# Gram products of two adapter pairs as four 64x64 blocks in a transformer layer with adapter feed-forwards

## The reference

```python
B, S, D, H = 16, 512, 256, 16            # batches, tokens, width, heads of 16
N, R = 8, 64                             # adapters and their inner width
def ffn(x):
    h = relu(einsum('btd,ndh->nbth', x, W_enc) + b_enc)       # h of all N adapters
    recon = einsum('nbth,nhd->nbtd', h, W_dec) + b_dec
    n = argmin(mean((recon - x) ** 2, axis=(2, 3)), axis=0)    # one adapter per batch
    mid = relu(x @ W_down[n] + b_down[n])
    return x @ W_base + b_base + mid @ W_up[n] + b_up[n]
x = x + 0.5 * ffn(layernorm(x))
x = x + attention(layernorm(x))          # rotary positions, softmax, float32
x = x + 0.5 * ffn(layernorm(x))
```

## Time and profile before

| | |
|---|---|
| Median of 3 runs | 1824.24 us (1820.42 to 1824.45) |
| The profiled execution | 1821.28 us, its span 1819.5 us |
| TensorE busy | 1719.4 us, 95% of the span |
| VectorE busy | 1270.7 us, 70% |
| ScalarE busy | 975.3 us, 54% |
| GpSimd busy | 501.8 us, 28% |
| Mean clock granted to TensorE | 0.969 of full speed |

### The profile page before, as it was taken

The page is one execution under the profiler, slowest core; times in us unless marked ns, Lnnn a source line. Parts: engine busy times, 40 slices in busy tenths (PEclk is TensorE's granted clock), DMA queues, the critical chain, the costliest instruction groups (busy, mean ns, idle before and its releaser), DMA issues.

```text
span 1819.5 us, 26356 instructions
## 1 busy us (share of the span) xinstructions
PE 1719.4 (95%) x9064; PEld 1004.2 (55%) x9064; DVE 1270.7 (70%) x2827; ACT 975.3 (54%) x1954; POOL 501.8 (28%) x665
## 2 busy tenths in 40 slices
PE   5478999999999999999999999999999999999966
PEld 4343555655555565656555565556556555654434
DVE  5558686877768686777868687776868777676521
ACT  2125565564747465564746556474746556474531
POOL 2414042230415133141513224141413304140101
PEclk9688999999999999999999999999999999999986
DMA  4343322333343123333322233333313333333000
GB/s 119 56 60 64 54 49 34 59 70 59 53 76 53 35 57 57 59 71 59 53 48 60 40 59 71 59 53 65 60 31 60 62 59 65 53 53 65 1 12 12
DMA packets 96716, 99.37 MB, mean 55 GB/s; under 512 B 19973, under 2 KB 88262, under 8 KB 96454
## 3 DMA queue, kind: packets, MB, share of 16 engines
q1 hardware_dynamic: 93830, 97.16, 30.9%
q10 hardware_dynamic: 2752, 0.54, 0.2%
HBM read 63.54 MB, written 33.55 MB: 53 GB/s over the span
## 4 chain that ended last, share of the span: by engine, by line
PE 85%; DVE 5%; ACT 4%; POOL 3%; issue 2%; DMA 1%; POOLq 0%; SPq 0%; ACTq 0%; DVEq 0%
PE ps L736 11%; PE ps L722 11%; PE ps L710 11%; PE ps L798 10%; PE ps L782 10%; PE ps L800 6%; PE ps L838 5%; PE ps L854 4%; PE ps L901 3%; PE ps L839 3%; PE ps L820 3%; PE ps L864 2%; ACT xn L961 2%; PE ps L767 1%; PE ps L885 1%
## 5 line engine op out<-in xcount | busy, mean ns | idle before, releaser
L1084 DVE TENSOR_REDUCE mx<-ps 128x1 f32<-128x512 f32 x1024 | 656.2, 683 | 240.6 <-PE ps L710 240.0
L936 ACT ACTIVATE pr<-ps 128x512 f32<-128x512 f32 x1024 | 556.6, 598 | 476.5 <-PE ps L722 474.0
L722 PE MATMUL ps<-stack 98*128 98x512 bf16 x1024 | 314.6, 384 | 9.2 <-DMA stack<-wu_mT 4.7
L710 PE MATMUL ps<-stack 96*128 96x512 bf16 x1024 | 311.4, 382 | 5.5 <-DVE mx L1084 4.9
L736 PE MATMUL ps<-pr,va 128*32 128x512 f32 x2048 | 248.7, 604 | 1.1 <-ACT pr L936 1.1
L722 PEld LDWEIGHTS ps<-stack 98*128 98x128 bf16 x1024 | 83.1, 98 | 181.1 <-issue 128.4
L1314 POOL CAST wdh<-wd_all 128x128 fp32r x32 | 9.5, 296 | 622.2 <-DVE adapter L1169 574.4
L710 PEld LDWEIGHTS ps<-stack 96*128 96x128 bf16 x1024 | 97.5, 98 | 141.1 <-DVE mx L1084 34.3
L1137 DVE SCALAR_TENSOR_TENSOR ps<-ps,wb,h 128x512 f32<-128x512 f32 x128 | 96.8, 756 | 99.4 <-PE ps L800 99.4
L986 ACT ACTIVATE h<-ps,benc 128x512 f32<-128x512 f32 x128 | 87.9, 687 | 99.1 <-PE ps L782 97.4
L800 PE MATMUL ps<-h,gram_w 128*128 128x512 f32 x256 | 130.5, 591 | 0.0
(11 more groups left out here) (150 smaller groups left out, 2987.5 us busy)
## 6 DMA issues: line engine op xcount, KB each, us to landing
stack<-scratch SPq DMA_DIRECT2D x384, 128.0 KB, 6.1
scratch<-parts SPq DMA_DIRECT2D x64, 384.0 KB, 2.6
xin<-in_L_attn_x_dram SPq DMA_DIRECT2D x16, 512.0 KB, 3.9
out_dram<-x SPq DMA_DIRECT2D x16, 512.0 KB, 8.7
stack<-wu_mT SPq DMA_DIRECT2D x128, 4.0 KB, 1.7
cst<-in_const_dram SPq DMA_DIRECT2D x1, 1024.0 KB
raw<-in_L_ffn_W_dec_dram ACTq DMA_DIRECT2D x1, 512.0 KB, 5.4
pr<-in_L_ffn_W_enc_dram SPq DMA_DIRECT2D x2, 256.0 KB, 7.6
```

The source lines that it names most:

```text
L710: pe.matmul(bank1[:, t % 2, :], stack[0][0:KB, hd, 128 * t:128 * t + 128], stack[1][0:KB, hd, :], start=True, stop=True).then_inc(s1_full. ...
L722: pe.matmul(bank2[:, a % 2, :], stack[1][:, 4 * g + a, 128 * t:128 * t + 128], stack[0][:, 4 * g + a, :], start=True, stop=True).then_inc( ...
L936: act.activation(held(b, n)[:, a, :], bank2[:, a % 2, :], ACT.Exp, scale=SCALE).then_inc(ex_done.sem, 1)
L1084: dve.tensor_reduce(mx[:, hd // 4 % 2, e:e + 1], bank1[:, t % 2, :], AX.X, ALU.max).then_inc(mx_done.sem, 1)
```

## The change

In the first feed-forward (and in the second of the last batch) the Gram products of pairs p - 1 and p, for p = 1 and 3, are issued together behind the decoder products of p, as four products of 64x64: the two members of the even pair on the diagonal of the array, the two of the odd pair off it. For that the Gram matrices of odd pairs are stored with their rows exchanged, and ScalarE writes a second copy of h for odd pairs, `turned`, whose halves are exchanged, ahead of h itself. One signal of 2 stands behind the fourth product. The second feed-forward of the other batches keeps the full product, for odd p with `turned`. `oT` gives up its own storage and lies in `raw[:, 2:4]`, for which the copy of raw's third block gets a wait. All five orders are rearranged; steps change places by up to some positions, and GpSimd's loop is cut at another point. The diff is cut: of the orders of TensorE, ScalarE and SyncE the parts that the text speaks of stand here, GpSimd's is whole, and VectorE's, in which few steps move, is left out.

```diff
 def tensor_order(stage):
 
     stage("s2", -1, 11, 0)
+    stage("en", +1, 0, 0)
     stage("s1", 0, 0, 0)
     stage("mt", -1, 3)
+    stage("s2", -1, 11, 1)
+    stage("en", +1, 0, 1)
+    stage("s1", 0, 0, 1)
     stage("en", +1, 0, 2)
-    stage("s2", -1, 11, 1)
-    stage("s1", 0, 0, 1)
-    stage("en", +1, 0, 3)
     stage("s2", -1, 12, 0)
     stage("s1", 0, 1, 0)
-    stage("pv", -1, 5)
+    stage("en", +1, 0, 3)
     stage("s2", -1, 12, 1)
     stage("s1", 0, 1, 1)
-    stage("gr", +1, 0, 0)
+    stage("pv", -1, 5)
     stage("s2", -1, 13, 0)
     stage("s1", 0, 2, 0)
-    stage("gr", +1, 0, 1)
+    stage("gr", +1, 0, 0)
     stage("s2", -1, 13, 1)
     stage("s1", 0, 2, 1)
-    stage("gr", +1, 0, 2)
+    stage("gr", +1, 0, 1)
     stage("s2", -1, 14, 0)
     stage("s1", 0, 3, 0)
-    stage("gr", +1, 0, 3)
     stage("dn", -2, 1)
+    stage("gr", +1, 0, 2)
     stage("s2", -1, 14, 1)
     stage("s1", 0, 3, 1)
+    stage("gr", +1, 0, 3)
     stage("pv", -1, 6)
+    stage("s2", -1, 15, 0)
     stage("mt", 0, 0)
-    stage("s2", -1, 15, 0)
     stage("s1", 0, 4, 0)
-    stage("up", -2, 1, 0)
     stage("cost", +1, 0)
     stage("s2", -1, 15, 1)
+    stage("up", -2, 1, 0)
     stage("s1", 0, 4, 1)
-    stage("up", -2, 1, 1)
+    stage("pv", -1, 7)
     stage("s2", 0, 0, 0)
     stage("s1", 0, 5, 0)
-    stage("pv", -1, 7)
+    stage("up", -2, 1, 1)
     stage("s2", 0, 0, 1)
     stage("s1", 0, 5, 1)
     stage("dn", +1, 0)
@@ -156,9 +158,9 @@
     stage("s2", 0, 2, 0)
     stage("s1", 0, 7, 0)
...
@@ -175,73 +177,72 @@
     stage("qk", +1, 0)
     stage("s1", 0, 9, 1)
     stage("tr", -1, 1, 0)
+    stage("qk", +1, 1)
     stage("s2", 0, 5, 0)
     stage("s1", 0, 10, 0)
-    stage("qk", +1, 1)
+    stage("va", +1, 0)
     stage("s2", 0, 5, 1)
     stage("s1", 0, 10, 1)
-    stage("va", +1, 0)
     stage("tr", -1, 1, 1)
+    stage("va", +1, 1)
     stage("s2", 0, 6, 0)
     stage("s1", 0, 11, 0)
     stage("pv", 0, 2)
     stage("s2", 0, 6, 1)
     stage("s1", 0, 11, 1)
-    stage("va", +1, 1)
     stage("en", -1, 1, 0)
+    stage("qk", +1, 2)
+    stage("mt", 0, 2)
     stage("s2", 0, 7, 0)
     stage("s1", 0, 12, 0)
-    stage("mt", 0, 2)
-    stage("qk", +1, 2)
     stage("en", -1, 1, 1)
+    stage("s2", 0, 7, 1)
     stage("qk", +1, 3)
-    stage("s2", 0, 7, 1)
     stage("s1", 0, 12, 1)
     stage("en", -1, 1, 2)
-    stage("pv", 0, 3)
     stage("s2", 0, 8, 0)
     stage("s1", 0, 13, 0)
     stage("en", -1, 1, 3)
+    stage("pv", 0, 3)
     stage("s2", 0, 8, 1)
     stage("s1", 0, 13, 1)
     stage("gr", -1, 1, 0)
     stage("s2", 0, 9, 0)
-    stage("tr", +2, 0, 0)
     stage("s1", 0, 14, 0)
     stage("gr", -1, 1, 1)
-    stage("tr", +2, 0, 1)
     stage("s2", 0, 9, 1)
+    stage("tr", +2, 0, 0)
     stage("s1", 0, 14, 1)
     stage("gr", -1, 1, 2)
+    stage("tr", +2, 0, 1)
     stage("s2", 0, 10, 0)
     stage("s1", 0, 15, 0)
-    stage("pv", 0, 4)
     stage("gr", -1, 1, 3)
     stage("s2", 0, 10, 1)
     stage("s1", 0, 15, 1)
-    stage("en", +2, 0, 0)
+    stage("pv", 0, 4)
     stage("cost", -1, 1)
-    stage("en", +2, 0, 1)
 
 
 def scalar_order(stage):
 
     stage("s2", -1, 11, 0)
     stage("mt", -1, 3)
+    stage("en", +1, 0, 0)
+    stage("s2", -1, 11, 1)
     stage("en", +1, 0, 1)
     stage("en", +1, 0, 2)
-    stage("s2", -1, 11, 1)
-    stage("en", +1, 0, 3)
...
@@ scalar_order @@
     stage("ro3", +1, 0)
+    stage("ro2", +1, 1)
     stage("mt", 0, 2)
     stage("s2", 0, 7, 0)
-    stage("ro2", +1, 1)
     stage("qk", +1, 2)
     stage("ro3", +1, 1)
     stage("en", -1, 1, 1)
...
@@ -387,40 +387,40 @@
 
 def gpsimd_order(stage):
 
-    stage("tl", -1, 1, 0)
-    stage("ro1", +1, 0)
-    stage("tl", -1, 1, 1)
-    stage("ro2", +1, 0)
-    stage("ro1", +1, 1)
-    stage("ro2", +1, 1)
-    stage("ro1", +1, 2)
     stage("rs", +2, 0)
     stage("ro2", +1, 2)
     stage("ro1", +1, 3)
-    stage("zs", -1, 1)
     stage("ro2", +1, 3)
+    stage("b0", +1)
     stage("pick", -1, 1)
-    stage("b0", +1)
     stage("zs", +2, 0)
     stage("pick", +2, 0)
     stage("rs", +2, 2)
     stage("rs", 0, 1)
+    stage("ro1", +2, 0)
+    stage("tl", 0, 1, 0)
+    stage("tl", 0, 1, 1)
+    stage("ro2", +2, 0)
+    stage("ro1", +2, 1)
+    stage("ro2", +2, 1)
+    stage("zs", 0, 1)
+    stage("ro1", +2, 2)
...
@@ sync_order @@
+    stage("mt", -1, 3)
     stage("mt", 0, 0)
     stage("lift", 0, 2)
     stage("lift", 0, 3)
     stage("store", -2)
+    stage("mt", 0, 1)
     stage("load", +2)
-    stage("mt", 0, 1)
+    stage("mt", 0, 2)
     stage("ro3", +1, 0)
     stage("ro3", +1, 1)
-    stage("mt", 0, 2)
     stage("lift", +1, 0)
     stage("lift", +1, 1)
-    stage("mt", 0, 3)
     stage("ro3", +1, 2)
     stage("ro3", +1, 3)
...
@@ -438,7 +438,7 @@
 
 def walk(order, do):
 
-    for number in range(-3, B + 2):
+    for number in range(-3, B + 3):
         def stage(name, ahead, *args):
             b = Batch(number + ahead)
             if 0 <= b.number < B and not (initial(b) and (name, *args) in BEGIN):
@@ -496,6 +496,7 @@
         stats, mv, rs = ([sb(f"{n}{s}", [128, T, w]) for s in range(3)] for n, w in (("st", 6), ("mv", 2), ("rs", 1)))
         shift = sb("shift", [128, T, 1])
         h = sb("h", [128, NP, S])
+        turned = sb("turned", [128, NP // 2, S])
         sx, sxx = ([sb(f"{n}{f}", [128, C]) for f in range(2)] for n in ("sx", "sxx"))
         r = [sb(f"r{f}", [128, NP]) for f in range(2)]
         z = [sb(f"z{f}", [128, N]) for f in range(2)]
@@ -527,7 +528,7 @@
         raw = sb("raw", [128, G, S])
         rz = sb("rz", [128, 2, H])
         on = xn[2]
-        oT = sb("oT", [128, C, S])
+        oT = raw[:, 2:4, :]
 
         scratch = [[nc.dram_tensor(f"scratch{o}{k}", [8, HD, 3, S], BF16, kind="Internal").ap() for k in range(4)]
                    for o in range(2)]
@@ -797,7 +798,21 @@
                     for w, x in ((w_dh, xh), (w_dl, xh), (w_dh, xl)):
                         pe.matmul(bank, w[:, c, 128 * p:128 * p + 128], x[f][:, c, :],
                                   start=(c == 0 and w is w_dh and x is xh), stop=False)
-                pe.matmul(bank, gram_w[:, p, :], h[:, p, :], start=False, stop=True).then_inc(gr_full[f].sem, 1)
+                if late_f:
+                    pe.matmul(bank, gram_w[:, p, :], turned[:, p // 2, :] if p % 2 else h[:, p, :], start=False, stop=True)\
+                        .then_inc(gr_full[f].sem, 1)
+                elif p % 2:
+                    products(b, f, p)
+
+            def products(b, f, p):
+
+                even, odd = dense_bank(b, f, p - 1), dense_bank(b, f, p)
+                low, high = slice(0, R), slice(R, 2 * R)
+                pe.matmul(even[low], gram_w[low, p - 1, low], h[low, p - 1, :], start=False, stop=True)
+                pe.matmul(even[high], gram_w[high, p - 1, high], h[high, p - 1, :], start=False, stop=True)
+                pe.matmul(odd[high], gram_w[low, p, high], turned[low, p // 2, :], start=False, stop=True)
+                pe.matmul(odd[low], gram_w[high, p, low], turned[high, p // 2, :], start=False, stop=True)\
+                    .then_inc(gr_full[f].sem, 2)
 
             def cost(b, f):
 
@@ -941,6 +956,8 @@
                 if m % 2 == 1:
                     if g == 0:
                         act.wait_ge(*on_done.at(b - 1, T - 1))
+                    if g == 2:
+                        act.wait_ge(*x2_done.at(b - 1, 1))
                     act.wait_ge(*pv_done.at(b, m))
                     act.copy(raw[:, g, :], bank_o).then_inc(raw_done.sem, 1)
 
@@ -983,6 +1000,9 @@
                 act.wait_ge(*(r_done[0].at(at_most_last(b + 2), NP - 1) if f else r_done[1].at(b - 3, p)))
                 bank = dense_bank(b, f, p)
                 act.wait_ge(*en_full[f].at(b, p))
+                if p % 2:
+                    act.activation(turned[0:R, p // 2, :], bank[R:2 * R, :], ACT.Relu, bias=benc[R:2 * R, p:p + 1])
+                    act.activation(turned[R:2 * R, p // 2, :], bank[0:R, :], ACT.Relu, bias=benc[0:R, p:p + 1])
                 act.activation(h[:, p, :], bank, ACT.Relu, bias=benc[:, p:p + 1]).then_inc(h_done[f].sem, 1)
 
             def down(b, f):
@@ -1054,7 +1074,8 @@
                     for e in range(2):
                         q = slice(R * e, R * e + R)
                         dve.tensor_scalar(wb2[q, p:p + 1], ps[q, 3, 10 * p + e:10 * p + e + 1], -1.0, None, ALU.mult)
-                        dve.tensor_copy(gram_w[q, p, R * e:R * e + R], ps[q, 2, 128 * p + R * e:128 * p + R * e + R])
+                        i = R * (1 - e) if p % 2 else R * e
+                        dve.tensor_copy(gram_w[i:i + R, p, R * e:R * e + R], ps[q, 2, 128 * p + R * e:128 * p + R * e + R])
                 link(dve.tensor_copy(power[:], power[:]))
                 dve.tensor_copy(power[:], power[:]).then_inc(s_ready, 1)
                 link(dve.tensor_copy(z[0][:], cidx[:].bitcast(I32)))
```

More of the change, by code:

```diff
@@ L240, in scalar_order @@
     stage("pv", -1, 5)
+    stage("s2", -1, 14, 1)
     stage("dn", -2, 1)
```

(3 more changed lines are left out.)

54 lines of the change are left out of this document (27 added, 27 removed).

## The result

The changed kernel takes 1843.05 us (median of 4 runs, 1841.01 to 1847.14) against 1824.35 us for the kernel before in the same comparison (1820.42 to 1825.46): a ratio of 1.0109, with a 95% interval of 1.0084 to 1.0134. The forecast was 1814 us and a range up to 1828 us. The change costs 19 us where I expected it to give 10. The profiled execution took 1841.26 us, its span 1839.5 us.

A forecast was written before the change was run, and what follows sets the result against it. TensorE's instruction stream was taken to bound the middle, a chain through several engines the head and tail. Blocks -17.6, copies +1.5, head and tail +6.4 gave -9.7 us: 1824.24 to 1814.5, rounded to 1814; range 1804 to 1828.

The forecast's parts named there:

- Orders and storage: Rearranged orders and oT in raw's last two blocks: charged nothing, with up to 0.4 us a batch (6 us) in the range.
- list of signs: Trace signs of a right or wrong forecast; wrong included TensorE idle before Gram products released by VectorE.
- the copies: Exchanged h on ScalarE: 128 activations at 0.60 us, 77 us in all; middle charged +1.5 us (0 to +15).
- the edges: Head, tail and batch 1's first feed-forward, where nothing covers added latency: +6.4 us (+3 to +9).
- a draw: Second feed-forward, encoder group 2: TensorE arrives and h 1 is done both at 7.6 us; charged 0.1 us a batch.
- The blocks: Gram pairs as four 64x64 products: 1.09 us instead of 1.72; 28 middle pairs save 17.6 us (11 to 24).
- Rival 3: Gram blocks don't share the array, one row half waits for the other: +16 us, about 1840; chance 0.06.
- rival 4: Gram blocks in one PSUM bank take turns, three rounds, 2.80 us instead of 1.72: +45 us, about 1869; chance 0.04.
- Head and tail: Both ends: late h and VectorE steps, head +2.0 and +0.9, tail +1.6 and +0.9, batch 1 +1; sum +6.4 us.
- rival 1: ScalarE late with h 1 at encoder group 2: 0.4 to 1.2 us a batch; at 0.5, about 1820; chance 0.20.
- rival 2: Copies paid in full at h 1 and h 3: 2.4 us a batch, +25 us, about 1849; chance 0.08.
- VectorE's joint step: VectorE's even-pair Gram step waits for the odd pair's blocks: 1.1 us before gr 2, covered in the middle, costed nothing.

The follow-up runs named there:

- e2: Kernel before with only the five new orders, full Gram products, no copies, oT in its own storage: 1837.14 us.
- e12: e2 with one exchange in VectorE's order, the second half of `lx` ahead of head 13's maxima: 1825.9 us.
- e3: Changed kernel with one exchange in VectorE's order, the second half of `lx` ahead of head 13's maxima: 1828.33 us.
- e8: e3 with full Gram products everywhere, copies kept, no blocks: 1847.45 us.
- e5: e3 without copies in the second feed-forward except in the last batch; results differ from the reference, only time counts: 1820.18 us.
- e1: Changed kernel's code (blocks, copies, oT in raw) with the five orders of the kernel before: 1874.22 us.
- e7: e3 with full products in the last batch's second feed-forward, copies kept: 1829.16 us.
- e11: e3 with full products and no copies in every second feed-forward, from a second store of odd Gram matrices; value bias folded into output bias: 1819.48 us.
- e4: e3 with TensorE's first value product of a batch moved back behind the second half of head 7's scores: 1849.41 us.
- e6: e3 with VectorE's first half of normalising x1 (`lx`) moved behind the output projection's first sum: 1831.6 us.

## Why the prediction was wrong

**The step that failed** is "Orders and storage", which I charged with nothing (and up to 0.4 us a batch in the range). I had walked the end of an iteration and checked that every consumer on TensorE comes 0.1 us or more after its input. The walk did not cover the two places that broke: VectorE's Gram step of group 0 behind `lx`, 1.1 us a batch by starts, and the maxima behind the output projection's sum, 0.44 by the view. The orders alone cost 12 us (`e2`); with one exchange in them 1.4, within the error, though the pace still shows 0.48 us a batch (`e12`). In the full change the same exchange is worth 15 us (`e3`). The rivals all named ScalarE or the array; none named VectorE, though 70% busy. The list of signs did name idle time released by VectorE, without a price.

**The second step**, mis-sized, is the copies: I charged 1.5 us in the middle plus most of the edges. They cost 21.5 us by the medians, 16.0 by the profiled executions (`e8` against `e12`). First the pitch, which I took as 0.60 us from an ordinary relu: it is 0.70, so an odd h comes 1.4 us late and not 1.2. Then the walk that ended in "a draw" for encoder group 2, at 0.1 us a batch: from the start of group 0 (991.93 in the trace after) ScalarE begins the copies at 6.07 us and not at 5.7, and h 1 ends at 8.16 and not at 7.6. The wait in the list is 0.27 us a batch, by starts it is 0.44, and dropping the copies of the second feed-forward gives 0.56 (`e5`). The reordering did take the wait of GpSimd's cast out of the way, as the walk had it: under the old orders the stall there is 1.0 us (`e1`), the number that I gave.

**The blocks** were right: 1.12 us a pair where I said 1.09, and 1.23 us a batch by `e8` against `e3` where 2 x 0.63 was forecast; 19.1 us in all by the medians, 16.0 by the profiled executions. Rival 3, a row half that waits for the other, and rival 4, blocks of a bank that take turns, are refuted by the starts within 0.02 us and by the distance to what follows: three rounds would have put the next score product 2.80 us behind. The rule of the Trainium skill, page "TensorEngine Tiling (Array Packing)", section "Restrictions and Gotchas", that different row tiles cannot access the same PSUM bank, does not show here for blocks that write different partition halves. The Trainium skill, page "PSUM — Partial Sum Buffer", section "PSUM bank collisions raise a hardware error", quotes the same rule and tells of an error for writes of row tiles to the same bank and the same 32-partition quadrant; the trace is in keeping with this second, narrower form.

**Head and tail**, +6.4 us in all: at the first output projection nothing was lost (-0.3 instead of +3.9 with batch 1), the tail lost 5.1 instead of 2.5, and the last iteration 2.8 more. The chain of the tail shows the links that I counted, but larger: from the first h to h 3 it is 3.1 us longer, where I had 1.6, and from there to the last Gram step 2.0, where I had 0.9. For the copies together `e7` against `e11` gives 4.7. The head does show the same links: the last Gram step of batch 0 starts at 38.71 us, before at 34.28, 4.4 later, where I had 2.9. But the next encoder's first h starts at 100.13 and before at 99.88. Between 38 and 60 us the granted clock (the third number from the end) differs, first before, then after:

```profile
38.00:60.00 22.00, 12.06 (x38) 8.65 (x38) 9.09 (x21) 0.68 (x1) 3.15 (x6) 0.51 0.08 24
38.00:60.00 22.00, 8.09 (x40) 5.50 (x40) 12.56 (x35) 0.68 (x1) 3.15 (x6) 0.81 0.09 24
```

`e12`, which makes no copy, has that Gram step at 38.43 and that h at 99.86, so there too a delay of 4 us is made up. That the clock alone makes it up is not shown. Nor is the -0.3 the price of the copies in general: in the traces of the nine kernels with copies in the first feed-forward the first output projection starts at 233.0 to 238.4 us, in the three with neither copies nor half steps (`e2`, `e12` and the kernel before) at 233.0 to 233.5.

**Rivals 1 and 2** had a true mechanism, h late at encoder group 2, whose size in the changed kernel is 0.27 us a batch of wait (0.44 by starts, rival 1's lower end), and in the old orders more than rival 2's price of 2.4 (3.0 us a batch of waits, `e1`). Neither explains the result by itself: by the waits in the middle, VectorE has 15.4 of the 18.4 us of TensorE that are listed. **VectorE's joint step**, which I costed at nothing for the cover of `dn`, had no wait in the middle.

Put together, each term being the difference of two kernels that stand one step apart:

| | medians, us | spans of the profiled executions, us | pace, us |
|---|---|---|---|
| before | 1824.5 | 1819.5 | 104.33 |
| orders without the misplaced `lx` | +1.4 | +7.4 | +0.48 |
| copies | +21.5 | +16.0 | +0.63 |
| blocks | -19.1 | -16.0 | -1.23 |
| the misplaced `lx` | +14.7 | +12.6 | +0.89 |
| after | 1843.0 | 1839.5 | 105.10 |

The first and the last term are of the orders, 16 to 20 us where I had nothing, and the last is one exchange of two neighbouring steps. With the edges counted to the copies, these were forecast at 7.9 us. The blocks, at -17.6, were right. So the forecast of -9.7 us missed by two terms, by 16 to 20 us in the orders and by 8 to 14 in the copies.

What stays open: whether some order frees the wait behind the output projection's sum (`e4` and `e6` did not), how much of the 15 us is GpSimd's hold on `lx` and how much its place in the order, what the moved transposes of TensorE add at that place, and what makes up the delay in the head.

## What to carry to other kernels

When orders are rearranged by hand together with a change, price them as an edit of their own: for each step that waits for a PSUM bank, write down what is queued in front of its releaser on that releaser's engine, over the whole iteration and not only where the change was made, and run the orders without the code. An engine at 70% busy can still be the one that is late, and a step placed behind one that has to wait is late even when its own input is long there. An extra operation on a lightly loaded engine is paid at each place where its result is the next input of the busiest one, so that a saving of 16 to 19 us can need 16 to 21 us of helpers; store the operand twice and make the copy only where the saving is.

## What the runs showed of the hardware

- Four float32 products of 64x64, on and off the diagonal of the array and two to a bank, start within 0.02 us and run side by side, in all 34 pairs: at the full clock 1.12 us a pair of full products instead of 1.72, the switch in and out included.
- Two activations that shift their data by 64 partitions start 0.70 us apart, and h behind them 0.70 too; an activation behind the ordinary relu starts 0.58 us later. Half the partitions save nothing, on ScalarE (0.68 to 0.69 us) or on VectorE (762 against 758 ns).
- A pair of VectorE operations over SBUF took 2.26 us beside GpSimd operations over SBUF and 0.88 without; the mean of one was 825 ns, and 522 ns when its place in the order changed.
